# Own places for O in chunk 0, the last chunk in stretches of 256, 128 and 128 queries, and fillers dealt by readiness, in an attention and quantized FFN kernel

## The reference

```python
Q, K, V = split(x @ WQ.T), split(x @ WK.T), split(x @ WV.T)
scores = jnp.where(causal, einsum('bhqd,bhkd->bhqk', Q, K) / sqrt(64), NEG)
e = jnp.exp(scores - max); attn = e / sum(e)
x = layernorm(x + join(attn @ V) @ WO.T)
# FFN: rms norm, 8-bit rounding by the row's absmax
x_q = activation_quant(simple_rms_norm(x))
y = layernorm(x + x_q @ (w_int8 * weight_scale).T + bias)
```

## Time and profile before

| | |
|---|---|
| median of three timed runs | 1059.05 us (1003.38 to 1085.48) |
| profiled execution | 1004.11 us, span 1002.6 us on core 2, the slowest |
| cores, spans | 994.9 to 1002.6 us |
| TensorE busy | 907.1 us (90%), 8267 matmuls recorded |
| ScalarE busy | 687.2 us (69%), of it 586.2 in 576 exponentials |
| VectorE busy | 519.0 us (52%) |
| GpSimd busy | 227.4 us (23%) |
| chain that ended last | TensorE 77%, DMA 8%, ScalarE 6%, issue 3%, VectorE 3% |

### The profile page before, as it was taken

The page is one execution under the profiler, slowest core; times in us unless marked ns, Lnnn a source line. Parts: engine busy times, 40 slices in busy tenths (PEclk is TensorE's granted clock), DMA queues, the critical chain, the costliest instruction groups (busy, mean ns, idle before and its releaser), DMA issues.

```text
span 1002.6 us, 22536 instructions; the slowest of 8 cores (994.9 to 1002.6 us)
## 1 busy us (share of the span) xinstructions
PE 907.1 (90%) x8267; PEld 409.9 (41%) x8416; DVE 519.0 (52%) x1263; ACT 687.2 (69%) x713; POOL 227.4 (23%) x290
## 2 busy tenths in 40 slices
PE   3894999999999989999999999999799999999863
PEld 1342444444444433434444444444344444444421
DVE  0110147744786327653127747762477523776675
ACT  0133666776877789999744566777577779999931
POOL 5021322231122121221223232232122211222101
PEclk9997999999999999999999999999899999999897
DMA  9999333250223141221154251144413210114212
GB/s 117 146 178 182 65 45 42 64 147 13 28 64 101 54 53 28 79 44 62 37 66 66 64 148 23 33 107 94 49 33 102 74 44 10 25 26 146 62 56 63
DMA packets 99289, 71.18 MB, mean 71 GB/s; under 512 B 70384, under 2 KB 88816, under 8 KB 99184
## 3 DMA queue, kind: packets, MB, share of 16 engines
q1 hardware_dynamic: 78368, 50.87, 20.5%
q0 software_dynamic: 20816, 18.88, 14.8%
HBM read 55.05 MB, written 16.78 MB: 72 GB/s over the span
## 4 chain that ended last, share of the span: by engine, by line
PE 77%; DMA 8%; ACT 6%; issue 3%; DVE 3%; POOL 1%; DVEq 0%; POOLq 0%; ACTq 0%; SPq 0%
PE ps L324 47%; PE ps L640 16%; PE ps L531 14%; ACT PT L559 5%; DMA WV<-wvt 4%; DMA QO<-OS 2%; DMA XT<-xt 1%; DVE OS L682 1%; DMA QT<-QB 1%; POOL PT L574 1%; ACT Q L844 1%; POOL WK L148 0%; POOL WQ L148 0%; DVE SM L678 0%; DVE Z L749 0%
## 5 line engine op out<-in xcount | busy, mean ns | idle before, releaser
L559 ACT ACTIVATE PT<-ps,SM 128x1024 bf16<-128x1024 f32 (+2 forms) x576 | 586.2, 1066 | 151.8 <-PE ps L531 149.8
L574 POOL TENSOR_TENSOR PT<-PT,MASK 128x256 bf16<-128x256 bf16 (+1 forms) x184 | 158.2, 867 | 506.0 <-ACT PT L559 505.8
L640 PE MATMUL ps<-VX,PT 128*128 128x65 bf16 x4352 | 235.1, 195 | 25.4 <-DVE OS L682 22.6
L640 PEld LDWEIGHTS ps<-VX,PT 128*128 128x128 bf16 x4352 | 179.2, 98 | 177.0 <-issue 141.9
L531 PE MATMUL ps<-QO,KT 64*128 64x512 bf16 (+1 forms) x1504 | 193.3, 325 | 10.9 <-ACT PT L559 10.2
L324 PE MATMUL ps<-XT,WK 128*128 128x512 bf16 x486 | 126.0, 386 | 23.8 <-DMA XT<-xt 22.4
L324 PE MATMUL ps<-W,QT 128*128 128x512 bf16 x477 | 128.6, 385 | 17.5 <-DMA QT<-QB 13.8
L324 PE MATMUL ps<-WO,QO 128*128 128x512 bf16 x474 | 127.0, 378 | 4.2 <-issue 1.7
L324 PE MATMUL ps<-XT,WQ 128*128 128x512 bf16 x485 | 124.6, 380 | 2.5 <-DMA WQ<-wqt 1.1
L324 PE MATMUL ps<-WV,XT 128*128 128x512 bf16 x489 | 124.1, 383 | 2.7 <-DMA WV<-wvt 1.4
L531 PEld LDWEIGHTS ps<-QO,KT 64*128 64x128 bf16 x1504 | 51.7, 94 | 182.2 <-issue 177.3
(11 more groups left out here) (50 smaller groups left out, 546.5 us busy)
## 6 DMA issues: line engine op xcount, KB each, us to landing
Z<-x SPq DMA_DIRECT2D x32, 512.0 KB, 4.4
y<-Z SPq DMA_DIRECT2D x32, 512.0 KB, 2.8
XT<-xt POOLq DMA_DIRECT2D x7, 1024.0 KB, 12.5
WK<-wkt POOLq DMA_DIRECT2D x4, 512.0 KB, 21.4
WQ<-wqt POOLq DMA_DIRECT2D x4, 512.0 KB, 24.6
WV<-wvt POOLq DMA_DIRECT2D x2, 1024.0 KB, 42.2
WO<-wot POOLq DMA_DIRECT2D x1, 2048.0 KB, 70.6
W<-w8t POOLq DMA_DIRECT2D x1, 2048.0 KB, 87.1
```

What stands on the lines that cost most here:

```text
L559: emit("s", lambda eng: eng.activation(dst, src, AF.Exp, bias=EB, scale=0.125).then_inc(sem["s"], 1))
L574: emit("g", lambda eng: eng.tensor_tensor(blk, blk, msk, ALU.mult).then_inc(sem["m"], 1))
L640: last = eng.matmul(ps[:, o_at + s_ * o_head + q * 65: o_at + s_ * o_head + q * 65 + 65], PT[:, pt0 + s_ * 512 + c0: pt0 + s_ * 512 + c0 + ...
```

## The change

It has five parts.

- **O of chunk 0.** The head pairs 2 to 7 of chunk 0 are evicted to O6 (the memory of Q16 and QB) and QT8, which are not in use yet, and have semaphores of their own. No eviction of chunk 0 waits for a transpose.
- **Stretches.** The second stretch of chunk 7 is cut in two of 128 queries. A unit there has four blocks of keys, 128 columns each, with a diagonal unit f. WO of tile 30 asks for the second stretch only, WO of tile 31 for the third.
- **Readiness of x transposed.** K, Q and V fillers ask for `xt_there`, set 12 us of the planner's clock after the load was issued.
- **Order and dealing.** Statistics, maximum and minimum of a half row are queued as soon as the half is there (`z_half`, `y_half`). In chunk 6 the WO fillers of the third tile stand ahead of the first K filler; in chunk 7 the FFN fillers stand further forward, the four Q fillers carried over from chunk 6 come behind them, tile 30 is taken into the chunk, and the last 8 gaps are left out of the dealing.
- **The end.** Only tile 31 comes after the last product. 57 matmuls on data at hand (`warm`) stand ahead of its WO (12) and of its FFN (45). The last scaling and store are done in two halves, one on each of two engines.

```diff
+        O6 = at("O6", [128, 1024], BF16, "q16")
...
             def ready():
-                if g not in tok_xt:
+                if g not in xt_there:
...
                 tok_xt[nxt] = (xt_load(xt_of(nxt), nxt, 0, 8,
                                        "xv" if nxt in in_v else "xt"),)
+                later(12000.0, lambda: xt_there.add(nxt))
...
-        subs += [(NCH - 1, 0, 2), (NCH - 1, 2, 2)]
+        subs += [(NCH - 1, 0, 2), (NCH - 1, 2, 1), (NCH - 1, 3, 1)]
...
+                    kinds = ["f"] + list(range(first_k % 4, first_k, 4))
...
+            if nq == 1:
+                keys = ([k0] + list(range(k0 % 4)) if kd == "f"
+                        else list(range(kd, kd + 4)))
+                return [(k, j * 128, q0 * 128, 128)
+                        for j, k in enumerate(keys)]
...
-            if i >= 2:
+            if su:
                 wait("v", tok_ot[(i - 2) // 8, (i - 2) % 8])
-            o0 = (i % 2) * 512
+            out, o_row, o0 = OS, 1024, (i % 2) * 512
+            if su == 0 and i >= 2:
+                out, o_row, o0 = ((O6, 1024, (i - 2) * 512) if i < 4 else
+                                  (QT8, 2048, (i - 4) * 512))
...
-            key = "ot%d" % (i % 2)
+            key = "ot%d" % (i % 2 if i >= 8 else i)
...
-            su = g if g < NCH - 1 else g + r // 2
+            su = g if g < NCH - 1 else g + max(0, r - 1)
...
+                z_half(n, dc)
                 if dc == 1:
                     z_stats(n)
...
+        def z_half(n, j):
+            z = zt(n, j * 512, j * 512 + 512)
...
+            for f in (stats, high, low):
+                bg.append((690.0, lambda f=f: emit("v", f)))
...
+            if n == 4 * NCH - 1:
+                wait("s", tok_sm2[n])
+                emit("s", lambda eng: eng.activation(
+                    zt(n, 0, 512), zt(n, 0, 512), AF.Identity,
...
+                store(n, bump("v"), 512, 1024)
+                store(n, t0, 0, 512)
...
+                if g == NCH - 1:
+                    order = [wo[0], wo[1], ff[0], wo[2], ff[1], wo[3],
+                             ff[2], ff[3]]
+                if g == NCH - 2:
+                    order = [wo[0], wo[1], wo[2]] + order[2:7] + order[8:]
...
-                mine += behind([4 * g, 4 * g + 1])
+                mine += carry
+                carry = []
+                tiles = [4 * g, 4 * g + 1, 4 * g + 2]
+                mine += behind(tiles)
...
-            todo = 2 * len(pairs[g])
-            gaps = [todo]
+            gaps = [2 * len(pairs[g]) - (8 if g == NCH - 1 else 0)]
...
-        main.extend(behind([4 * NCH - 2, 4 * NCH - 1]))
+        main.extend(behind([4 * NCH - 1]))
+        idle = [0]
+        def warm():
+            if idle[0] == 0:
+                wait("t", tok_exp[len(units) - 1], tok_exp[len(units) - 2])
+            idle[0] += 1
+            emit("t", lambda eng: eng.matmul(
+                ps[:, 0:512], WO[:, 0:128], WO[:, 0:512], start=True,
+                stop=True, skip_group_check=True))
         while main or st["open"] or timed or bg:
             if step() == 0.0:
-                spend(100.0)
+                if main and idle[0] < (12 if len(main) > 2 else 57):
+                    warm()
+                    spend(216.0)
+                else:
+                    spend(100.0)
```

More of the change, by code:

```diff
@@ L111, in build_nc @@
             sem["wv%d" % j] = e(nc.semaphore("sem_wv%d" % j))
+        for j in range(8):
             sem["ot%d" % j] = e(nc.semaphore("sem_ot%d" % j))
@@ L448, in build_nc @@
         proj_left = {g: 24 for g in range(NCH)}
+        xt_there = {0, 1}
         def next_xt(g, t):
@@ L468, in xt5_load @@
             tok_xt[5] = (xt_load(XT0, 5, 0, 8, "xv"),)
+            later(12000.0, lambda: xt_there.add(5))
         subs = [(g, 0, 4) for g in range(NCH - 1)]
-        subs += [(NCH - 1, 0, 2), (NCH - 1, 2, 2)]
+        subs += [(NCH - 1, 0, 2), (NCH - 1, 2, 1), (NCH - 1, 3, 1)]
         units = []
@@ L483, in build_nc @@
                     kinds = ["d0", "d1", "d2"] + list(range(first_k))
+                elif nq == 2:
+                    kinds = ["e"] + list(range(0, first_k, 2))
                 else:
-                    kinds = ["e"] + list(range(0, first_k, 2))
+                    kinds = ["f"] + list(range(first_k % 4, first_k, 4))
                 for kd in kinds:
@@ L551, in emit_s @@
             s0 = (u % 2) * 1024
-            if kd in ("d2", "e"):
-                c0, nc_ = (256, 256) if kd == "d2" else (0, 384)
+            if kd in ("d2", "e", "f"):
+                c0, nc_ = {"d2": (256, 256), "e": (0, 384),
+                           "f": (0, 128 * len(mm))}[kd]
                 dst = ap(PT, pt0 + c0, (4096, 128), (512, 2), (1, nc_))
@@ L586, in pv_lists @@
                 return [(k0, 1, 128)], [(k0, 0, 0), (k0 + 1, 1, 256)]
+            if nq == 1:
+                if kd == "f":
+                    return ([(k, 0, 128 + k * 128) for k in range(k0 % 4)],
+                            [(k0, 0, 0)])
+                return [(kd + j, 0, j * 128) for j in range(4)], []
             if nq == 2:
@@ L682, in f @@
                 eng.tensor_tensor(
-                    ap(OS, o0, (1024, 128), (64, 2), (128, nq), (1, 64)),
+                    ap(out, o0, (o_row, 128), (64, 2), (128, nq), (1, 64)),
                     ap(ps, o_at, (4096, 128), (o_head, 2), (65, nq), (1, 64)),
@@ L692, in o_out @@
             c0 = ((g * 8 + hp) % 16) * 512 + q0 * 128
-            key = "ot%d" % (i % 2)
+            key = "ot%d" % (i % 2 if i >= 8 else i)
             emit("y", lambda eng: eng.dma_start_transpose(
                 ap(QO, c0, (8192, 128), (128, nq), (1, 128)),
-                OS[:, o0:o0 + nq * 128]).then_inc(sem[key], 16))
+                out[:, o0:o0 + nq * 128]).then_inc(sem[key], 16))
             tok_ot[su, hp] = bump(key, 16)
             if hp == 7:
-                later(5500.0, lambda: state["ot_all"].add(su))
+                later(5500.0 if su < len(subs) - 1 else 3800.0, lambda: state["ot_all"].add(su))
         tok_x, tok_store, tok_sm, tok_q16, tok_qt8 = {}, {}, {}, {}, {}
@@ L713, in sm, with rows @@
             return SM[:, s0 + c0:s0 + c1]
-        def rows(t_h, n):
+        def rows(t_h, n, c0=0, c1=D):
             g, r = n // 4, n % 4
-            return ap(t_h, (g // 4) * S * D + ((g % 4) * 512 + r * 128) * D,
-                      (D, 128), (1, D))
+            return ap(t_h, (g // 4) * S * D + ((g % 4) * 512 + r * 128) * D
+                      + c0, (D, 128), (1, c1 - c0))
         def x_load(n):
@@ L912, in done @@
                 tok = bump("v")
+                y_half(n, dc)
                 if dc == 1:
@@ L957, in out @@
         def out(n, on_act):
-            if on_act:
+            if n == 4 * NCH - 1:
+                wait("s", tok_sm2[n])
+                emit("s", lambda eng: eng.activation(
+                    zt(n, 0, 512), zt(n, 0, 512), AF.Identity,
+                    bias=sm(n, 32, 33), scale=sm(n, 31, 32)).then_inc(
+                        sem["s"], 1))
+                t0 = bump("s")
+                wait("v", tok_sm2[n])
+                emit("v", lambda eng: eng.tensor_scalar(
+                    zt(n, 512, 1024), zt(n, 512, 1024), sm(n, 28, 29),
+                    sm(n, 31, 32), ALU.subtract, ALU.mult).then_inc(
+                        sem["v"], 1))
+                store(n, bump("v"), 512, 1024)
+                store(n, t0, 0, 512)
+            elif on_act:
                 wait("s", tok_sm2[n])
@@ L976, in store @@
             emit("y", lambda eng: eng.dma_start(
-                rows(y_h, n), zt(n)).then_inc(sem[key], 16))
+                rows(y_h, n, c0, c1), zt(n, c0, c1)).then_inc(sem[key], 16))
             tok_store[n] = bump(key, 16)
```

47 lines of the change are left out of this document (19 added, 28 removed).

## The result

The changed kernel took 989.1 us (988.5 at the least), the kernel before, timed beside it, 1003.4 at the least. The ratio is 0.985, with a 95% interval of 0.982 to 0.988: 1.5% faster, which is within the 2% called "the same". The forecast said 978. The range of 968 to 992 holds the result; "over 2% faster" was wrong.

What follows compares the result with a forecast made beforehand. TensorE's two long waits and chunk 7's exponentials on ScalarE, then a dependent chain, were taken as bounds. 1002.6 - 15.3 - 7.7 + 6.5 - 12.9 = 973.2; slowest core 2, FFN data 1, time over span 1.5: 978 us, range 968 to 992.

Steps and rivals of the forecast that it cites:

- Part 1: Chunk 0: own places for O remove a 12.5 us eviction wait and 2.8 us lost at half clock, 15.3 us gained.
- Rival B: Chunks 0 and 1: late transposes or loads make WO or K wait, costing up to half the 15.3; 986 us, chance 0.07.
- Part 2: Order around the last load of x transposed, before chunk 7: 5.1 us wait and 2.6 at half clock go, 7.7 gained.
- Part 3: Chunk 7 with its second stretch cut in two: more filler work, one Q activation and a burst cost 6.5 us.
- 24 x 0.18 = 4.3: Chunk 7: 24 more filler pairs ahead of the last product at 0.18 us each, 4.3 us added.
- the 1 us beside it for a burst: Chunk 7: tile 30's last FFN filler, 16 matmuls in one piece ahead of the last two units, adds 1 us.
- a chunk that passes 150: Sign against the chunk 7 forecast: the chunk takes over 150 us, where about 145 was expected.
- rival A: Chunk 7: each short score matmul pays its whole weight load; 998 us, or 991 at about 81 ns each; chance 0.09.
- down to the wire once or twice: Halves of statistics let FFN fillers be dealt earlier, their data arriving just in time once or twice; 1 us added.
- Rival C: Small FFN waits of 1 to 2 us in four or five tiles, last FFN at half clock; 986 us, chance 0.12.
- Part 4: Behind the last exponential: one row tile instead of two, last FFN at full clock; 30.8 us against 43.7, 12.9 gained.
- The two adjustments for the slowest core and the waits of the FFN: Added to the summed span: about 2 us for the slowest core, 1 us for FFN data arriving just in time.

Runs made afterwards that it cites:

- places_alone: The kernel before with only the places of its own for O in chunk 0 added; 989.3 us in one execution.
- q_first: ffn30_even with the carried Q fillers ahead of the first WO tile in chunk 7, as before the change; 975.5 us, ratio 0.975.
- tile30_behind: The changed kernel with WO and FFN of tile 30 both behind the last product; 984.1 us.
- ffn30_even: ffn30_old_order with the work of chunk 7 dealt over all its gaps, not all but the last eight; 973.5 us, ratio 0.972.
- ffn30_old_order: The changed kernel with tile 30's FFN behind the last product and, in chunks 0 to 6, statistics queued, charged and ordered as before the change; 976.8 us, ratio 0.978.
- even_alone: The changed kernel with chunk 7's work dealt over all its gaps, and nothing else but the choice of bank; 983.0 us.

## Why the forecast was right and wrong, point by point

**Part 1: right.** Forecast 15.3 us, measured 15.5; WO of chunk 1 begins at 121.20, forecast 121. The expected next hindrance (transposes that pile up) did not come: the longest wait on an eviction is 1.0 us. Rival B falls. The size is again that of the slowest core: in the kernel before, chunk 0 took 57.8 to 61.6 us on the eight cores (mean 59.7), so the mean gain is 13.6.

**Part 2: right on the core it was read from.** 7.7 forecast, 7.1 measured. What I did not look at is how much the core mattered. In the kernel before, the second wait on x transposed lasted from 2.0 to 5.1 us on the eight cores, and chunk 6 from 125.3 to 130.2. After, it is 123.1 on all. The mean gain is 4.7, or 3.2 against places_alone.

**Part 3: the mechanism right, the size wrong.** The step that failed is "24 x 0.18 = 4.3", and the 1 us beside it for a burst. The chunk by its filler pairs (two matmuls of 512 columns each) ahead of the last product:

| kernel | pairs: 256 / both 128 | 256 queries, us | both 128, us |
|---|---|---|---|
| before (256 and 256) | 52 / 52 | 63.8 | 74.8 |
| q_first | 56 / 64 | 67.4 | 73.0 |
| tile30_behind | 63 / 49 | 69.2 | 72.0 |
| ffn30_even | 63 / 57 | 69.2 | 72.0 |
| ffn30_old_order | 63 / 57 | 70.0 | 75.1 |
| after | 65 / 63 | 70.5 | 82.6 |
| even_alone | 67 / 61 | 74.0 | 72.9 |

The slope of 0.18 us a pair came from two head pairs. The lighter was at the floor that ScalarE sets (busy 8.15 of 8.30 us), where pairs are free; the heavier was above it (TensorE busy 9.09 of 9.20). A line through one point on either side of a bend gives a slope that holds nowhere. In the last stretches pairs are nearly free up to 4 a head pair (49 or 57 of them 72.0 us, 61 and 64 of them 73.0), and above that each costs its own time. Two neighbouring head pairs of the kernel after show it, with 4 and with 5 filler pairs:

```profile
885.70:890.00 4.30, 4.30 (x69) 2.21 (x68) 2.85 (x7) 4.24 (x6) 1.06 (x2) 1.00 0.52 198
890.00:894.80 4.80, 4.80 (x76) 2.45 (x73) 3.19 (x7) 4.15 (x5) 0.82 (x2) 1.00 0.71 200
```

TensorE is busy without a gap in both; with the fifth pair ScalarE begins to wait: half a microsecond for one pair, whose two matmuls take 0.43.

So 24 pairs were not one quantity. 13 of them went into the stretch of 256 queries, where TensorE was already busy 60.1 of 63.8 us: +6.7 us. That is 0.5 a pair if all of it is put down to them, which is not shown. Two more Q activations lie in this stretch as well, 2.5 us of ScalarE (busy 63.2 us, before 60.4); with fillers of half the columns it still took 66.1 to 68.4; and no run took just these pairs out. The other 11 are in the last two stretches: +7.8, and this is a matter of where they stand: 64 pairs dealt in fours take 73.0 there, 63 in bunches 82.6. 6.3 us are the one piece of tile 30's FFN. I had named that piece and its light surroundings and given it 1 us. I should have priced it as an ordered wait: 16 matmuls at half clock, 5.3 us, plus 1.6 for their data, in front of the last scores, is 6.9 without cover, because ScalarE has nothing else left to do. The kernel before showed the price already, in a stretch that I did not price: its last head pair, with 16 FFN matmuls in pieces of 10 and 6 among the last units, took 12.1 us, where the seven ahead of it took 8.3 to 9.2.

```profile
946.80:958.90 12.10, 10.93 (x107) 5.43 (x106) 6.46 (x15) 9.76 (x10) 1.81 (x2) 0.72 0.25 49
```

The sign of being wrong that I had set for part 3, a chunk that passes 150, is met (153.0 on this core).

The short score matmuls were priced rightly: eight of 128 columns take 0.40 us in the row at 944.96, where 0.39 was the price of four of 256. The Trainium skill's 81 ns each ("TensorE: Matmul & The Clock Gate", section "Back-to-back issue gap") would be 0.65 for the eight; here the measurement decides, and rival A falls. (The 0.15 us a unit for switching between groups in rival A's sum came from no row.)

**Chunks 1 and 5, +5.0: a term of 1 us.** I had costed the statistics in halves and the new charges as "down to the wire once or twice". Set back, they give the whole loss back, so the new order is the cause; how it costs the time is shown only in part. TensorE's waits are 2.8 us in chunk 1 (1.1 before) and 1.7 in chunk 5 (none before), none over 1.0, and of the new ones just one in each chunk, 0.7 us, is for the FFN's data. Rival C had small waits in many places and the last FFN at half clock, with 986 as its time; of all rivals it comes nearest, but its waits of 1 to 2 us on the FFN's data are not there, and the larger part of the miss is chunk 7.

**Part 4: right but for the clock.** From the last exponential to WO 3.7 us (forecast 4.0), from WO to Q 10.7 (10.9), from Q to the last FFN 5.1 (5.0), from there to the end 12.7 (10.9). The last is the 1.7 us of the half clock. My reason against it was a row that showed a clock of 1.00 over 3.3 us without work on one core. The row behind it, which I left out of account, is this:

```profile
974.00:976.50 2.50, 0.00 (x0) 0.00 (x0) 1.98 (x8) 0.06 (x1) 0.70 (x1) 0.53 0.00 0
```

TensorE had stopped at 970.7 and the clock fell soon after 974. What counts is the clock at the next matmul, and one row over idle time on one core did not tell it: behind a stop of 2.5 us core 1 of the changed kernel ran its last FFN at full clock, and the seven others did not. The same FFN in the kernel before would have warned me, as it took 5.30 us on three cores of eight.

**The sum.** On the profiled spans 987.4 - 973.2 is 14.2 us: part 3 7.9, chunks 1 and 5 5.0, part 4 1.5, part 2 0.6, part 1 -0.2, chunks 2 to 4 and the start -0.7. The two adjustments for the slowest core and the waits of the FFN, 3 us, took up part of it.

## What to carry to other kernels

Where two engines are both near their limit, price added work by the engine that it lands on, head pair by head pair, and not by a slope between two points of one stretch. In an in-order queue look at what stands behind the last piece: work whose data are just arriving belongs behind the last product, where it cost 0.5 to 1.0 us, and not in one piece ahead of it, where it cost 6.3 us. Small changes to a planner's charges reorder the whole program: keep them out of stages that the change isn't for, and read a gain on all cores before counting the one where it is largest.
